# Count matrix of a graph kernel: source blocks against windows of 512 instead of 256 targets, one-hot vectors built part by part

## The reference, cut to what matters

```
L0: out[dst] += h[src] @ W + b, divided by the number of edges into dst
L3, three times: h = h + relu(sum over edges(norm * (h @ W.T)[src]) + b)
src is uniform; dst = int(6250 * u ** 2), so low targets have far more edges
```

## Time and profile before

| | |
|---|---|
| median of 3 runs | 7363.7 us (7361.1 to 7378.8) |
| span of the profiled execution | 7357.1 us |
| keys block and before | 0 to 775 us |
| adjacency block | 775 to 1565 us |
| layers | 1565 to 7357 us |

### The profile page before, as it was taken

The page is one execution under the profiler, slowest core; times in us unless marked ns, Lnnn a source line. Parts: engine busy times, 40 slices in busy tenths (PEclk is TensorE's granted clock), DMA queues, the critical chain, the costliest instruction groups (busy, mean ns, idle before and its releaser), DMA issues. The chain is left out here.

```text
span 7357.1 us, 136936 instructions
## 1 busy us (share of the span) xinstructions
PE 5543.0 (75%) x29811; PEld 3798.0 (52%) x29813; DVE 4289.6 (58%) x15050; ACT 1780.6 (24%) x3520; POOL 3246.1 (44%) x3354
## 2 busy tenths in 40 slices
PE   3511788869766666666666599999999998899999
PEld 3511344447533433433433366666666666687877
DVE  7887777761278787777777544444444444322222
ACT  0010688850122222222222222222222221100000
POOL 0100500000077777777777177777777775000000
PEclk9975778879888888888888677777777776899999
DMA  1070222236444444444445122222222223466666
GB/s 37 1 237 8 100 100 102 100 126 264 150 93 92 92 92 92 92 92 92 92 92 88 26 47 47 47 47 47 47 47 47 47 47 36 171 262 235 256 241 226
DMA packets 1052581, 764.66 MB, mean 104 GB/s; under 512 B 868977, under 2 KB 978241, under 8 KB 1032914
## 3 DMA queue, kind: packets, MB, share of 16 engines
q1 hardware_dynamic: 664738, 483.03, 21.7%
q0 software_dynamic: 131808, 243.11, 14.1%
q10 hardware_dynamic: 255904, 37.09, 3.0%
HBM read 657.77 MB, written 143.22 MB: 109 GB/s over the span
## 5 line engine op out<-in xcount | busy, mean ns | idle before, releaser
L1869 POOL DMA_INDIRECT rows<-node_rows_wide,idx_ring x1612 | 1537.0, 953 | 501.5 <-issue 426.0
L1869 POOL DMA_INDIRECT rows<-node_rows,idx_ring x1612 | 1522.6, 945 | 492.4 <-issue 491.0
L1918 PE MATMUL ps_sum<-hots,act_ring 128*97 128x128 f32 x3224 | 571.4, 333 | 756.9 <-DVE hots L1903 716.4
L1918 PEld LDWEIGHTS ps_sum<-hots,act_ring 128*97 128x97 f32 x3224 | 463.5, 200 | 1059.2 <-DVE accT L1912 1033.2
L1381 PE MATMUL ps_conv<-conv_rows,adj_ring 128*128 128x288 bf16 x7497 | 941.3, 288 | 45.5 <-DVE conv_rows L1340 21.9
L1912 DVE TENSOR_TENSOR accT<-accT,ps_sum 97x128 f32 (+1 forms) x3224 | 908.8, 282 | 5.0 <-PE ps_sum L1918 4.0
L1381 PEld LDWEIGHTS ps_conv<-conv_rows,adj_ring 128*128 128x128 f16 x7497 | 738.0, 99 | 233.5 <-issue 24.2
L1945 PE MATMUL ps_e<-w1e,aT 128*128 128x384 f32 x1612 | 799.1, 632 | 18.5 <-DVE aT L1981 18.5
L1143 PE MATMUL ps_blocks<-end_hot 128*128 128x256 bf16 x2800 | 673.9, 409 | 112.3 <-DVE end_hot L1123 104.1
L1123 DVE TENSOR_TENSOR end_hot<-iota_h,lanes 128x1536 bf16<-128x1536 bf16 x700 | 631.1, 963 | 156.0 <-ACT ps_blocks L1171 85.0
L2026 PEld LDWEIGHTS ps_w<-w2w,hid 97*128 97x128 f32 x3224 | 478.3, 228 | 469.3 <-issue 390.8
(11 more groups left out here) (341 smaller groups left out, 5879.1 us busy)
## 6 DMA issues: line engine op xcount, KB each, us to landing
adj_ring<-adjacency SPq DMA_DIRECT2D x144, 2176.0 KB, 7.8
adjacency<-panels SPq DMA_DIRECT2D x588, 128.0 KB, 1.7
idx_ring<-sorted_pairs SPq DMA_DIRECT2D x1612, 1.0 KB
attr_ring<-sorted_attr ACTq DMA_DIRECT2D x1612, 16.0 KB
rows<-node_rows_wide,idx_ring POOLq DMA_INDIRECT x1612
attr_ring<-sorted_attr SPq DMA_DIRECT2D x1612, 8.5 KB
rows<-node_rows,idx_ring POOLq DMA_INDIRECT x1612
sorted_attr<-in_edge_attr SPq DMA_DIRECT2D x5, 5000.0 KB
```

The source lines that it names most:

```text
L1869: g.indirect_dma_start(out=rows[:, r, j, 0:width], out_offset=None, in_=table, in_offset=bass.IndirectOffsetOnAxis(ap=idx, axis=0)).then_i ...
L1918: last = pe.matmul(ps_sum[0:M, r % 2, j, :], what(r, j), hots[:, r % 2, j, :], start=True, stop=True)
```

## The change

A window is 512 targets, so 13 windows, and a bucket is a panel. There are 49 x 13 = 637 buckets; the bound of parts is 1562 + 637 = 2199, rounded to 2208 (138 turns), and 20 gathers instead of 24. The key has one bit less of window and one more of target. `count_chunk` makes 49 + 3 + 13 one-hot rows a chunk. One-hots are f16 and contiguous: each part has two TENSOR_SCALAR instructions, 128 elements for the source and 512 for the target, each comparing the iota with a per-partition scalar in SBUF (f32) of `lane_ring`. That ring of 8 turns is filled by GpSimd, 4 turns with one copy. TensorE's matmul has 512 columns, and TensorE, not VectorE, waits for the emptied bank, every 4 parts, against a register of which it loads 16 a turn. The loop bodies hold 8 turns. The heavy cells are computed by VectorE in the keys block, after the sorted keys are sent off; GpSimd sends them after its last copy. ScalarE's and SyncE's work is the same in count and size. The diff, cut to its core:

```diff
-WD = 256
-
-ENDS = 1 + WD // P
+QW = 4
+WD = QW * P
 NW = -(-NP // WD)
-WB = 5
+WB = 4
+LOG_WD = 9
 BUCKETS = NB * NW
+LB = NB + QW - 1
 NB_BITS = 64
 BASE = 0x20000000
 GK = 16
 HALF = GK // 2
+LR = 8
+LH = LR // 2
 LOG_P = 7
 PARTS = E // P + BUCKETS
 Q2 = -(-PARTS // GK)
 T2 = Q2 * GK
 HB = 2
 HK = 4
-NK = -(-NW // 2)
+HOT = P + WD
+NK = NW
...
-            lanes = tmp("lanes", [P, ENDS, TP], BF16)
-            iota_h = tmp("iota_h", [P, P, HK], BF16)
+            lanes = tmp("lanes", [P, 2, TP])
+            iota_h = tmp("iota_h", [P, WD], F16)
+            heavy_cell = tmp("heavy_cell", [P, NK, HV, WD], F16)
...
-                    v.tensor_copy(onehots[:, NB, :], dst_half[:, cols])
+                    for k in range(1, QW):
+                        v.tensor_scalar(onehots[:, NB + k - 1, :], dst_quarter[:, cols], float(k), None, ALU.is_equal)
                     for k in range(NW):
-                        last = v.tensor_scalar(onehots[:, NB + 1 + k, :], dst_w[:, cols], float(k), None, ALU.is_equal)
+                        last = v.tensor_scalar(onehots[:, LB + k, :], dst_w[:, cols], float(k), None, ALU.is_equal)
...
+                def mark_heavy(v):
+
+                    for k in range(NK):
+                        cols = PANEL_COLS[k]
+                        for n in range(HV):
+                            last = v.tensor_scalar(heavy_cell[:, k, n, 0:cols], iota_h[:, 0:cols], float(WD * k),
+                                                   heavy_to[:, n:n + 1], ALU.add, ALU.is_equal)
+                    last.then_inc(heavy_cells.sem, 1)
...
-                end_hot = btmp("end_hot", [P, HB, GK // HK, ENDS, P, HK], BF16)
-                flat_hot = end_hot[:, :, :, :, :, :].rearrange("p r n c l k -> p r n (c l) k")
-                src_hot, dst_hot = flat_hot[:, :, :, 0:P, :], flat_hot[:, :, :, P:P + WD, :]
-                panels = btmp("panels", [P, NK, 2 * WD], F16)
-                target = btmp("target", [P, 2 * WD])
-                heavy_cell = btmp("heavy_cell", [P, NK, HV, 2 * WD], F16)
-                ps_b = ctx.enter_context(nc.psum_tensor("ps_blocks", [P, BANKS * 2 * WD], F32))
+                end_hot = btmp("end_hot", [P, HB, GK, HOT], F16)
+                lane_ring = btmp("lane_ring", [P, 2, LR * GK])
+                panels = spare[:, 0:NK * WD // 2].bitcast(F16).rearrange("p (k c) -> p k c", c=WD)
+                ps_b = ctx.enter_context(nc.psum_tensor("ps_blocks", [P, BANKS * WD], F32))
...
-                        for n in range(GK // HK):
-                            if n * HK % HALF == 0:
-                                empty = v.value_load(part_panel[:, dyn(q * GK + n * HK + HALF - 1, 1)], min_val=1,
-                                                     max_val=PANELS + 1)
-                                past(v, block_mm, (q - HB) * GK + n * HK + HALF)
-                                v.sem_inc(passed_v.sem, 1)
-                                v.wait_ge(emptied.sem, empty)
-                            lane = lanes[:, :, dyn(q * GK + n * HK, HK)].unsqueeze(2)
-                            v.tensor_tensor(end_hot[:, r, n, :, :, :],
-                                            iota_h[:, :, :].unsqueeze(1).to_broadcast([P, ENDS, P, HK]),
-                                            lane.to_broadcast([P, ENDS, P, HK]), ALU.is_equal).then_inc(ends_hot.sem, 1)
-                    turns(v, [(hots, 0)], Q2, HB)
+                        if r % LH == 0:
+                            v.wait_ge(lanes_in.sem, turn * (LR // LH) + r // LH + 1)
+                        for j in range(GK):
+                            if j % HALF == 0:
+                                past(v, block_mm, (q - HB) * GK + j + HALF)
+                            at = r * GK + j
+                            v.tensor_scalar(end_hot[:, r % HB, j, 0:P], iota_h[:, 0:P], lane_ring[:, 0, at:at + 1],
+                                            None, ALU.is_equal)
+                            last = v.tensor_scalar(end_hot[:, r % HB, j, P:HOT], iota_h[:, :],
+                                                   lane_ring[:, 1, at:at + 1], None, ALU.is_equal)
+                            if j % HK == HK - 1:
+                                last.then_inc(ends_hot.sem, 1)
+                    turns(v, [(hots, 0)], Q2, LR)
...
                     def count(q, turn, r):
 
                         at = nc.values_load_multi_w_load_instructions(
-                            part_col[:, dyn(q * GK, GK)], [PE], min_val=0, max_val=BANKS * 2 * WD - WD,
+                            part_col[:, dyn(q * GK, GK)], [PE], min_val=0, max_val=(BANKS - 1) * WD,
                             skip_runtime_bounds_check_because="a window's columns in one of the banks")[1]
+                        empty = nc.values_load_multi_w_load_instructions(
+                            part_panel[:, dyn(q * GK, GK)], [PE], min_val=1, max_val=PANELS + 1)[1]
                         for j in range(GK):
                             if j % HK == 0:
+                                pe.sem_inc(passed_t.sem, 1)
+                                pe.wait_ge(emptied.sem, empty[j + HK - 1])
+                            if j % HK == 0:
                                 past(pe, ends_hot, q * (GK // HK) + j // HK + 1)
-                            pe.matmul(ps_b[:, dyn(at[j], WD)], src_hot[:, r, j // HK, :, j % HK],
-                                      dst_hot[:, r, j // HK, :, j % HK],
+                            pe.matmul(ps_b[:, dyn(at[j], WD)], end_hot[:, r % HB, j, 0:P], end_hot[:, r % HB, j, P:HOT],
                                       start=False, stop=True, skip_group_check=True).then_inc(block_mm.sem, 1)
-                    turns(pe, [(count, 0)], Q2, HB)
+                    turns(pe, [(count, 0)], Q2, LR)
...
+                    def lane_turns(q, turn, r):
+
+                        if r % LH == 0:
+                            past(g, ends_hot, (q - LH) * (GK // HK))
+                            g.tensor_copy(lane_ring[:, :, r * GK:(r + LH) * GK],
+                                          lanes[:, :, dyn(q * GK, LH * GK)]).then_inc(lanes_in.sem, 1)
+                    turns(g, [(lane_turns, 0)], Q2, LR)
...
-                    g.iota(target[:, :], [[1, 2 * WD]], base=0, channel_multiplier=0,
-                           allow_small_or_imprecise_dtypes=True).then_inc(made.sem, 1)
-                    g.wait_ge(made.sem, MADE + ADJ_MADE + 1)
-                    for k in range(NK):
-                        for n in range(HV):
-                            last = g.tensor_scalar(heavy_cell[:, k, n, 0:PANEL_COLS[k]], target[:, 0:PANEL_COLS[k]],
-                                                   heavy_to[:, n:n + 1], float(-2 * WD * k), ALU.subtract, ALU.is_equal)
-                        last.then_inc(heavy_cells.sem, 1)
...
+                    g.wait_ge(heavy_cells.sem, 1)
                     for k in range(NK):
                         cols = PANEL_COLS[k]
-                        g.wait_ge(heavy_cells.sem, k + 1)
                         g.dma_start(adj_h[k * P:(k + 1) * P, NB * cols:SB * cols].rearrange("p (n c) -> p n c", n=HV),
```

More of the change, by code:

```diff
@@ L101 @@
 CB = SB // NC
-PANEL_COLS = tuple(min(2 * WD, NP - 2 * k * WD) for k in range(NK))
+PANEL_COLS = tuple(min(WD, NP - k * WD) for k in range(NK))
 assert CB * NC == SB and PANEL_COLS[NK - 1] == P
-assert (NB - 1) % BANKS == 0 and TP <= 2 * SN and NK <= 13 and KEYS > E + P and NW <= 1 << WB and COLS % OCN == 0
+assert (Q2 - 1) // LH * LH * GK + LH * GK <= TP and (NB - 1) % BANKS == 0 and TP <= 2 * SN and NK <= 13 and KEYS > E + P and NW <= 1 << WB and COLS % OCN == 0
 ZR = 8
@@ L181, in graph_kernel @@
         ends_h = nc.dram_tensor("panel_ends", (NB, NK), I32, kind="Internal").ap()
-        adj_h = nc.dram_tensor("adjacency", (NK * P, SB * 2 * WD), F16, kind="Internal").ap()
+        adj_h = nc.dram_tensor("adjacency", (NK * P, SB * WD), F16, kind="Internal").ap()
         x = sbuf("x", [P, NB, D])
@@ L319, in graph_kernel @@
         heavy_cells = sem("heavy_cells")
+        lanes_in = sem("lanes_in")
         heavy_in = sem("heavy_in")
@@ L779, in place_buckets @@
                     v.wait_ge(onehot_used.sem, OCN)
-                    step(v, v.tensor_scalar(of_upper[0:NB + 1, :], of_window[0:NB + 1, :], float(NB), None, ALU.is_equal))
-                    link(v, v.tensor_copy(counts[0:NB + 1, 0:NW], ps_c[0:NB + 1, 0:NW]))
-                    link(v, v.tensor_scalar(of_lower[0:NB + 1, :], of_upper[0:NB + 1, :], -2.0, 1.0, ALU.mult, ALU.add))
+                    for k in range(1, QW):
+                        step(v, v.tensor_scalar(of_quarter[k][0:LB, :], of_window[0:LB, :], float(NB + k - 1), None,
+                                                ALU.is_equal))
+                    step(v, v.tensor_scalar(of_quarter[0][0:LB, :], of_window[0:LB, :], float(NB), -2.0, ALU.is_ge,
+                                            ALU.mult))
+                    link(v, v.tensor_copy(counts[0:LB, 0:NW], ps_c[0:LB, 0:NW]))
```

(21 more changed lines are left out.)

86 lines of the change are left out of this document (40 added, 46 removed).

## The result

The changed kernel takes **8011.1 us** in the median of 4 runs (8001.5 to 8014.1), against 7366.5 us for the kernel before in 4 runs: a ratio of 1.087, 95% interval 1.085 to 1.089. The profiled execution has a span of 8008.8 us, 652 more than before.

The account below looks back on a forecast made before the run. Before, no engine fills the stage (sums 607 to 677 us, plus waits); after, VectorE bounds it: 984 + 12 + 15 + 10 + 6 = 1027, +237, keys block -26, so +211: span 7568, median 7575 us, range 7480 to 7710.

Parts of the forecast that it names:

- One-hots: VectorE, adjacency stage: two instructions a part cost 0.446 us, x 2208 = 984 us (944 to 1023), against 607 before.
- Rival A: VectorE's one-hots: the scalar's load hides, a part takes 0.306 us, stage about 730 us, kernel about 7278; 11%.
- TensorE's matmuls: TensorE, adjacency stage: 512 columns take 0.216 us at 2.4 GHz, 0.43 at 1.2; mostly hides, adding 12 us (0 to 62).
- rival B: TensorE, adjacency stage: it is the bound, 512 columns costing 0.43 us at either clock; kernel 7624 us; 6%.
- The registers: TensorE, per turn: registers and waits beside the matmuls cost 0.4 us before, put at 0.8 with twice the registers.
- The wait on TensorE: TensorE waiting for the emptied bank, adjacency stage: costs 0, since VectorE is late next.
- Loop, copies, filling: Adjacency stage: VectorE's loop jumps 15 us (0 to 20), GpSimd's copies 10 (0 to 60), pipeline filling and emptying 6 (4 to 8).
- the lower clock: TensorE, adjacency stage: at 1.2 GHz 0.5 us more a turn; 28 us, over half absorbed by the ring, leaving 12.
- Heavy cells, keys block, layers: Heavy cells hide in VectorE's wait for gathered keys, 0; keys block -26 us (-22 to -28); layers unchanged.
- terms 2 and 3: Adjacency stage: TensorE's matmuls and registers add 12 us (term 2), its wait for the emptied bank adds 0 (term 3).
- the prediction is wrong if VectorE is not the bound: Sign for the adjacency stage: VectorE was to be busy nearly all of its 1027 us with TENSOR_SCALAR.

Follow-up runs that it names:

- four_values: The changed kernel, but TensorE loads and bounds-checks only the 4 values it waits against, not all 16 of a turn; stage 970.1 us, ratio to before 1.026.
- vector_waits: The changed kernel, but VectorE waits for the emptied bank every 8 parts, as before the change; stage 972.4 us, ratio to before 1.029.
- numbers_for_scalars: VectorE waits for the bank as before the change, and the changed kernel's one-hots compare with a fixed number instead of a scalar from SBUF; stage 806.5 us.
- before_checked: The kernel before, with only the 16 column addresses that TensorE loads each turn bounds-checked; stage 1488.9 us, ratio 1.083.
- interleaved_layout: The changed kernel with VectorE waiting for the bank and one-hots made four parts at a time, interleaved, windows still 512 targets; stage 1014.2 us.

## Why the prediction was wrong

The figure was 7575 us with a range of 7480 to 7710, and 8011 is above it. Step by step:

1. **One-hots**: the mechanism right, the size 5% high. Predicted 0.446 us a part within 0.428 to 0.463, measured 0.425; 984 us against 938, just under the lower bound of 944. The four-fold rate is there, the scalar costs what L933 said, and the rival that hides the load is out. Rival A's own time was not: with the pair at 0.304 us, where A had 0.306, the stage is 806 where A had 730; ScalarE's 637 us sit just below, and VectorE waits for it.
2. **TensorE's matmuls**: the rate is right (0.217 and 0.427 us a matmul at the two levels, predicted 0.216 and 0.43), and rival B is out. **The registers are the step that failed**: "with twice the registers I put 0.8" a turn. The 0.4 of before was the busy time of 16 matmuls over 16 times their spacing; it holds the end of each burst, and not what the registers cost. That cost was hidden, since the queue loads while the matmuls sent off before still run, and the trace of before had the price in TensorE's queue, 1.26 us a load. The second load took 1.4 to 1.5 us, and the tests, which the prediction does not mention, 16 x 0.29 = 4.6. So it was 6 us a turn for 0.4, and a stream of 10.4 us beside VectorE's 6.8, where the prediction had 4.3 to 7.6 beside 7.1 and called it hidden.
3. **The wait on TensorE**: "**0**, since VectorE is late next". That VectorE would be next was the error that followed. In the trace it is TensorE's queue, and VectorE waits 483 us for it. For the wait itself, 0 was right as far as was tried: four_values keeps it and loses nothing against vector_waits. What is queued behind the waiting instruction ("queued behind it are its own weight loads and matmuls") was asked only for the wait, and not for the instructions that prepare it.
4. **Loop, copies, filling**: 31 us and 12 for the lower clock, on top of the one-hots. In vector_waits, where VectorE does decide, 972 - 938 leaves 34. Near in sum, but by luck in its parts: VectorE waits 20 us for TensorE and 7 for ScalarE there, which leaves some 6 for the jumps (15), GpSimd's copies (10) and the filling (6) together. The copies take 0.37 us each, 13 in all. No run isolates the term for the clock.
5. **Heavy cells, keys block, layers**: the heavy cells hide as forecast, with 28 us of VectorE's wait for the gathered keys left behind them; keys block -20 for -26, and the missing 6 us were not traced. The layers are 11 us longer, of which no part of the change speaks; two runs of one kernel differ by as much (7361 to 7379).

The sum of the prediction without the failed step, then: 1027 against 972 for the kernel that has the rest of the change, and 7357 + 183 - 20 = 7520 for the span, within the range (an estimate, with the stage of another chip). The time missed by 436 us. The registers and tests of TensorE cost 478 where terms 2 and 3 had 12 and 0, and the rest of the stage was forecast 55 too high, which hid a part of the error. The sentence "the prediction is wrong if VectorE is not the bound" named the case, without a chance for it: rival B gave TensorE the bound for its columns, and nobody gave it for its own instruction stream.

It could have been read in the trace of before. There the panel number's line on VectorE, and the columns' line on TensorE, are:

```profile
L1117 DVEq FUSED_REGOPS  x608: 57/190/216, 774.9 to 1557.4; - x152
L1117 DVEq TENSOR_LOAD <-accT x350: 297/378/866, 774.3 to 1557.1; - x175
L1117 DVEq SEQ_ASSERT  x350: 23/23/39, 775.1 to 1557.7; - x175
```

```profile
L1137 PEldq TENSOR_LOAD <-accT x175: 1102/1255/3672, 774.7 to 1558.9; - x175
```

One test for each value where no reason to skip is given, 350 for 350, none on L1137; and the price of a load. The busy times leave all of these out, as the page of the profile says of register instructions.

## What to carry to other kernels

An engine has two sums, its busy time and its instruction stream, and only the first is in a table of busy shares; for a loop that loads registers, add up the rows of the engine's queue per turn before moving anything onto it. Load and test only the values that are used (4 tests for 16 saved 480 us here), leave waits on registers with the engine whose queue has room, and take "issue" ahead of a burst as a reason to look at that engine's own queue. Where a row names another engine for a wait, count whether that engine had not long been done. And look in the trace that an added load is still there, before the run is taken for an answer.

## What was not expected of the hardware

- A register load on TensorE's queue takes 1.36 us for 16 contiguous values, 1.26 for 4 at a step of 16 bytes and 2.28 for 8 at a step of 8 bytes; a tested value costs 0.29 us there. On VectorE's queue before, one value took 0.38.
- In numbers_for_scalars GpSimd's copy into the lane ring took 1.84 us in the mean of the 30 between 800 and 1500 us, 7.28 in the row below and 9.7 at most, where vector_waits has 0.37 and 0.55 at most:

```profile
1195.27 7.28 POOL L1196 COPY lane_ring<-lanes 128x128 f32 x1 [23.94 <-DVE end_hot L1136]
...
1216.63 0.29 POOL L1196 COPY lane_ring<-lanes 128x128 f32 x1 [14.08 <-DVE end_hot L1136]
```

The long one ended at 1202.55, when VectorE's unbroken row of one-hots had ended at 1202.39. The Trainium skill, SBUF — State Buffer, section on terms, says that VectorE and GpSimd lock a shared pair of ports for the whole of an instruction, and that the loser is blocked wholly. This trace agrees with the blocking, but here it lasted through some 23 pairs one after another and not one instruction. Why the instructions with a scalar from SBUF let GpSimd in between them was not tried.
- The granted clock over the stage was 0.74 in the changed kernel, 0.97 in vector_waits, 0.60 (from 800 to 1500 us) in before_checked and 1.00 in interleaved_layout. TensorE paused 4 to 5 us between bursts in the first and third, mostly under 1 us in the second and not at all in the last. But that does not order all of them: the kernel before had 0.80 with only 112 us of idle time in the stage, and vector_waits 0.97 with 374. What set the clock is open.
